# The same instructions in another order of turns on all five engines, with another map of PSUM banks

## The reference

```python
# tokens of an image: stem, deformable convolution, 25 positions of 192
h = leaky_relu(batchnorm(conv2d(x, stem_w, stem_b, 4)))          # 96 x 21 x 21
offset = conv2d(h, off_w, off_b, 4)                              # 32 x 5 x 5
h = leaky_relu(batchnorm(deform_conv(h, offset, dcn_w, dcn_b)))  # 192 x 5 x 5
h = concatenate([h as 25 tokens, txt], axis=1)                   # 102 tokens of 192
# attention with 12 heads of 16, integers by fake_quant, softmax by integer exponent and power of two
h = h + attn(layernorm(h))
# feed-forward, 192 -> 768 -> 192, gelu
h = h + gelu(layernorm(h) @ w_in.T + b_in) @ w_out
```

## Time and profile before

| | |
|---|---|
| median of 3 runs | 1013.89 us (1013.72 to 1017.25) |
| profiled execution, span | 1014.5 us |
| TensorE busy | 880.8 us (87%) |
| VectorE busy | 876.0 us (86%) |
| ScalarE busy | 779.8 us (77%) |
| GpSimd busy | 266.9 us (26%) |
| mean granted TensorE clock | 0.951 |
| transfers | 53.42 MB, mean 53 GB/s |

### The profile page before, as it was taken

One profiled execution on the slowest core, in us unless ns is written; L12 is line 12 of the kernel. 1 busy time (PEld: TensorE's weight loads), 2 busy tenths in 40 slices (PEclk: granted clock), 3 DMA queues, 4 the chain that ended last, 5 costly groups with the idle time before them and its releaser, 6 DMA issues. The chain is left out here.

```text
span 1014.5 us, 18281 instructions
## 1 busy us (share of the span) xinstructions
PE 880.8 (87%) x5594; PEld 539.9 (53%) x5594; DVE 876.0 (86%) x1695; ACT 779.8 (77%) x1529; POOL 266.9 (26%) x248
## 2 busy tenths in 40 slices
...
PEclk9987769999999999999999999999999999998678
...
DMA packets 132628, 53.42 MB, mean 53 GB/s; under 512 B 105103, under 2 KB 131413, under 8 KB 132437
## 3 DMA queue, kind: packets, MB, share of 16 engines
...
## 5 line engine op out<-in xcount | busy, mean ns | idle before, releaser
L563 POOL TENSOR_TENSOR ee_sb<-ee_sb,rs_sb 128x1020 f32<-128x1020 f32 x64 | 157.2, 2464 | 379.1 <-DVE rs_sb L1059 379.1
L1195 PE MATMUL bank<-hats_sb,ht_sb 127*96 127x400 f32 (+1 forms) x384 | 147.9, 522 | 1.7 <-DVE hats_sb L921 1.7
L1327 PE MATMUL bank<-w_out_sb,ge_sb 128*102 128x192 f32 x768 | 138.8, 331 | 10.9 <-DVE y_sb L1096 6.9
L1327 PEld LDWEIGHTS bank<-w_out_sb,ge_sb 128*102 128x102 f32 x768 | 120.3, 168 | 31.6 <-issue 17.8
L921 DVE TENSOR_TENSOR hats_sb<-hats_sb 126x1600 f32<-126x1600 f32 x64 | 127.2, 1987 | 0.7
L648 ACT ACTIVATE hats_sb<-bank 126x400 f32<-126x400 f32 (+1 forms) x256 | 108.2, 523 | 0.3 <-PE bank L1181 0.3
L727 ACT ACTIVATE a_sb<-scores,sc_sb 128x1020 f16<-128x1020 f32 x64 | 71.1, 1111 | 39.2 <-PE scores L1279 39.2
L1195 PEld LDWEIGHTS bank<-hats_sb,ht_sb 127*96 127x96 f32 (+1 forms) x384 | 58.7, 166 | 72.6 <-issue 69.3
L734 ACT ACTIVATE sq_sb<-rm_sb,sc_sb 128x1020 f32<-128x1020 f16 x64 | 73.5, 1148 | 18.2 <-DVE rm_sb L1031 18.0
L572 POOL TENSOR_TENSOR xshift_sb<-mv_sb,xshift_sb 102x4 f32<-102x4 f32 (+1 forms) x33 | 11.0, 333 | 279.9 <-DVE ve_sb L961 278.5
L1242 PE MATMUL bank<-xt_sb,w_in_sb 128*128 128x408 f32 (+1 forms) x204 | 82.0, 527 | 1.0 <-ACT xt_sb L667 1.0
...
## 6 DMA issues: line engine op xcount, KB each, us to landing
...
q_sb<-qb_sb SPq DMA_DIRECT2D x192, 12.8 KB, 1.9
...
```

Source lines behind the costliest of these rows:

```text
L563: nc.gpsimd.tensor_tensor(EE[b][:], EE[b][:], RS[b][:].unsqueeze(2).to_broadcast([128, RT, TOK]), ALU.mult).then_inc(scaled_done, 1)
L1195: last = mm(dst, HT[0:rows, t.i, j, :], HATS[t.i][0:rows, 1 + j, :], start=(j == 0 and not odd), stop=(j == NCH - 2 and odd == 1))
L1327: last = mm(bank[t.banks[0]][0:TOK, 0:D], GE[:, f, t.i * TOK:(t.i + 1) * TOK], WOUT[:, f, :], start=(f == 0), stop=(f == FT - 1))
```

## The change

Each engine has the same set of turns, with the same groups and images meeting in a round, in another order. The lags are written from another origin (the last is 55 instead of 59, PREP0 has -60). In full rounds the order changes as follows; images are those of one round.

The string is replaced as a whole, with the banks:

```diff
-dve.MXB.54 act.XH2.17 pe.INT.9 dve.QQG.55 act.XH2.16 dve.MXC.54 pe.PV3.16 act.V.12 dve.REM.55
...
-dve.PREP2.44
+dve.PW.52 act.HAT.8 pe.PV3.16 dve.PR.52 act.OC.17 dve.RES.55 pe.HTT.6 act.INT.11 dve.LS2.55 sp.QD.20
...
+dve.PR.49 pe.INT.5 act.PV2.13 dve.HAT.42
-BANKS = dict(FFA=(1, 0, 4, 2), STEM0=(5, 4), STEM1=(0, 4), HTT=(5,), OFF=(1,), OFS=(0,), HAT=(5, 0),
-             INT=(3, 2), DCN=(4,), LN1X=(2,), LN2X=(0,), V0=(4, 1), V1=(4, 3), FQ0=(5, 2),
-             FQ1=(0, 4), PV2=(1,), PV3=(4,), FFN0=(5, 3), FFN1=(0, 1), FFN2=(4, 2), FF2=(3,))
+BANKS = dict(FFA=(0, 4, 3, 1), STEM0=(4, 5), STEM1=(3, 5), HTT=(0,), OFF=(4,), OFS=(4,),
+             HAT=(3, 0), INT=(2, 4), DCN=(5,), LN1X=(4,), LN2X=(2,), V0=(2, 3), V1=(1, 3),
+             FQ0=(0, 5), FQ1=(2, 4), PV2=(1,), PV3=(5,), FFN0=(2, 3), FFN1=(0, 1), FFN2=(5, 4),
+             FF2=(2,))
```

More of the change, by code:

```diff
@@ L96 @@
-act.INT.4 pe.INT.6 dve.MXB.51 act.XH2.14 dve.MXC.51 pool.NRM.14 pe.HTT.3 act.LN2X.15 dve.DST.51
-sp.PT.14 dve.BND.51 act.V.9 pe.PV3.13 dve.MAX.50 act.SQ.11 dve.QQ.51 pe.PV2.12 act.LN2X.14
-dve.PREP2.44
+dve.PW.52 act.HAT.8 pe.PV3.16 dve.PR.52 act.OC.17 dve.RES.55 pe.HTT.6 act.INT.11 dve.LS2.55 sp.QD.20
+dve.QKC.48 act.PV2.16 pe.SC.15 pool.RS1.4 dve.HATW.46 act.HTT.7 dve.HAT.45 pe.STEM1.4 act.OC.16
+dve.PV3.54 act.INT.10 dve.HATW.45 pe.SC.14 dve.RES.54 act.SC.15 dve.HAT.44 pe.INT.8 sp.LX.8
+act.VC.15 dve.PV3.53 act.STEM.5 pe.HTT.5 dve.LS2.54 dve.RES.53 act.STEM.4 pe.V1.12 dve.HATW.44
@@ new lines @@
+act.HTT.6 dve.PV3.52 pool.NRM.9 act.SC.14 pe.LN2X.19 dve.LN2A.52 act.INT.9 dve.PREP1.40 sp.SD.16
+pe.SC.13 dve.RES.52 act.INT.8 dve.LS2.53 act.XH2.19 pe.LN2X.18 dve.LS2.52 act.XH2.18 dve.LN2.52
+pe.OFF.4 dve.MAX.51 act.LN2X.19 dve.VE2.52 act.LN2X.18 pe.LN2X.17 dve.MXB.51 act.XH2.17 sp.DCN.16
+dve.MXC.51 pe.DCN.8 pool.NRM.8 act.SQ.15 dve.DST.51 dve.MAX.50 act.V.13 pe.LN2X.16 dve.BND.51
+act.XH2.16 dve.MXB.50 pe.SC.12 act.VC.14 dve.QQ.51 dve.MXC.50 act.VC.13 pe.FFA.16 dve.QQG.51
+sp.YO0.28 act.LN2X.17 dve.DST.50 pe.OFS.4 act.SC.13 dve.EP.51 act.HTT.5 pe.FFN0.16 dve.PREP2.44
```

16 lines of the change are left out of this document (added).

## The result

The changed kernel takes 1028.15 us, median of 4 runs (1025.83 to 1033.8), against 1013.81 us (1011.69 to 1017.25) for four runs of the kernel before: a ratio of 1.0148, 95% interval 1.0114 to 1.0182. The forecast was 1011 us with a range to 1024 us; the time is that of rival 1 (1025 us) and 3 us more. The profiled executions lie closer together than the medians: the changed kernel's was the fastest of its four (1025.83 us, span 1023.7 us), the kernel before's the slowest (1017.25 us, span 1014.5 us), so the traces hold 9 us of the 14 us.

A forecast was written before the change was run, and what follows sets the result against it. A loop between VectorE and ScalarE, closing once per group, was taken to bound the kernel: +0.3 - 0.8 + 0.4 us a group, -1.3 us over 13 groups, -1 us for both ends, so 1011 us; range 1000 to 1024 us.

The forecast's parts named there:

- rival 1: GpSimd's RS1 late in every group, XH1 waits 1.4 us, period 56.15 us: 1025 us; chance 0.22.
- the term for XH1's wait: ScalarE's first XH1 of a group waits for GpSimd's RS1: 0.4 us taken, between 0 and 1.4 us.
- the upper bound of 1.4 us: XH1's wait if RS1's power must sit out EXP too, with RS1 ending at about 579.6 us.
- second half of the loop: LOG.36 to the next QKC: FQ1 ahead of PV2 on ScalarE gives -0.8 us, bounds -0.6 and -1.0 us.
- the +0.3 us for the scores: QKC to LOG.36: VectorE reaches MAX.36 sooner and waits for scores, 0.3 us a group, between nothing and 0.8 us.
- my fourth rival: TensorE falls to its lower clock in other places, some us either way; the clock or something else: chance 0.06.
- HAT.0 starts at 38.9 us: At the start, sooner offset rows are hidden by VectorE's weight preparation; HAT.0 still at 39 us.
- The end: At the end, MXC ahead of QQG may save VectorE 0.5 us.
- HATW of the group's first image: On VectorE, beside GpSimd's NRM.35: HATW.40 loses 0.1 to 1.5 us, none of it on the loop.
- a sign of trouble: A new steady wait on TensorE for a bank or for the gelus would show the forecast wrong.
- The banks at nothing: The new map of PSUM banks costs nothing; every turn finds its bank drained in time, except FF2.
- Rival 2: RS1 and scores in time, freed turns count in full, period 54.45 us: 1003 us; chance 0.30.

The follow-up runs named there:

- experiment 5: Changed kernel with the FF2.28 turn of VectorE moved behind EXP.34 instead of ahead of it: 1008.14 us, ratio 0.9956 to the kernel before.
- experiment 2: Kernel before with VE1 moved behind PR.32, ahead of QQ.35 and EXP.34, as the new order has it: 1049.2 us, ratio 1.0339.
- experiment 1: Changed kernel with VE1 put back directly behind LN1 on VectorE: 1001.72 us, ratio 0.9884 to the kernel before.
- experiment 3: Kernel before with FQ1 directly behind FQ0 on ScalarE, ahead of the PV2 turn: 1010.3 us, ratio 0.9993.
- experiment 8: Kernel before with OFS of group 0 ahead of WDF on GpSimd at the start: 1011.48 us, ratio 0.9973.
- experiment 6: Changed kernel with VE1 half-way back, behind REM.34 and ahead of DST.35: 1004.97 us, ratio 0.9921 to the kernel before.

## Why the prediction was wrong

**The step that failed** is the term for XH1's wait: "Between these ends I take 0.4 us, since the FF2 turn between QQ and EXP.34 reads a PSUM bank and gives GpSimd a gap of 0.3 us." It measured 1.35 us, at the upper bound of 1.4 us that the same passage had. The chain up to there was right: VE1 4.3 us later (4.34 us), and nothing of the margin left if GpSimd isn't let through. What failed is that the FF2 turn would let the power in. FF2 was there, 0.35 us long, the power was issued under it, 0.17 us ahead of EXP.34, and it wasn't let in: it took 3.64 us in all of 13 groups. And I had thought of EXP alone as what holds it, where it was held over four instructions. The upper bound came out right by luck in its cause: it had RS1 done 8.6 us after LN1 and its reader due at 7.2 us, and they came at 8.89 and 7.6 us. Held by EXP alone, RS1 would have ended at about 7.8 us and cost 0.3 us, as in experiment 5. Why a power issued just ahead of EXP waits for four instructions, and one issued just behind its start (experiments 2 and 5) for one, stays open.

**The other terms.** The prediction's second half of the loop rests on QKC of group 10 at 648.56 us, taken from the distance of the two LN1 turns; the trace has it at 648.21 us, so that half was 27.22 us in the round read, not 27.57 us. From QKC to LOG.36 the loop took 28.09 us before and takes 27.79 us in experiment 1 and 28.21 us in the changed kernel (means over 12 groups, those of the other half over 11), so the +0.3 us for the scores wasn't there; VectorE comes to MAX.36 no sooner (12.43 and 12.37 us after QKC). From LOG.36 to the next QKC it took 27.59 us, in experiment 1 26.56 us: -1.03 us, where I had -0.8 us. But the reason was wrong: experiment 3 gives nothing for FQ1's place, and from 200 to 900 us QKC waited for FQ1 only in the round that I had read. That the number is near is luck. The gain arises along the stretch, 0.29 us up to LN1, 0.40 us from there to XH1, 0.34 us to QKC. Changed kernel against experiment 1, that half takes 28.10 - 26.56 = 1.54 us more. That adds up: 0.12 - 1.03 + 1.54 = +0.63 us a group, measured +0.66 us.

**Without a price** was TensorE's clock, my fourth rival, "worth some us either way". It isn't free of the rest: the wait that XH1 hands on brings it. In the new order that is worth some 3.4 us by the profiled execution (5 us, uncertain by 5 us, by the runs), in the old one (experiment 2) about as much as XH1's lateness itself (1.2 against 1.1 us a group). Rival 1 had no such term, but +0.3 us for the scores that mostly wasn't there, and -0.8 us for -1.03 us; its period was to rise by 0.9 us and rose by 0.66 us, and the medians differ by 5 us more than the profiled executions. So its 1025 us lies near the 1028 us partly by luck.

**The ends and the cover.** HAT.0 starts at 38.9 us, as forecast, and experiment 8 confirms that this start is hidden. The end cost 1.2 us instead of giving 0.5 us. HATW of the group's first image fell from 2.56 to 2.00 us, as said, without an effect. FF2's first turn does wait behind the gelus (7.8 us in 12), which I had named as a sign of trouble; in experiment 1 it waits 8.7 us in 13 and the kernel is 1.2% faster, so it is covered. The banks at nothing: the changed kernel's waits of TensorE for a bank are those for FF2's single one (5.7 us in 12, in experiment 1 18.4 us in 26), which the prediction had excepted, and for LN1X's (5.5 us in 9, before 4.3 us in 12). In the old order the map costs 7.9%.

**The rivals.** Rival 2's world is experiment 1: 54.45 us and 1003 us forecast, 54.35 us and 1001.72 us measured. Rival 1's is the changed kernel. The Trainium skill (SBUF — State Buffer, Who interferes with whom) let me derive rival 1 from its strict rule, and its direction was right. But I applied the rule with EXP.34 issued ahead of the power, and in the changed kernel the power is issued first, by 0.17 us, and waits all the same, while EXP keeps its 1.27 us. So the rival came true on a condition that didn't. Where EXP is issued first, in experiments 2 and 5, the power waits for that one instruction, if it ends 0.87 to 1.04 us after it is let in, and these traces agree with the rule; the last multiply of experiment 6, issued behind EXP too, waits over four. I gave rival 1 0.22, against a single favourable argument that no row of the trace had shown; the row that it needed, a GpSimd instruction let in by a turn as short as FF2's, wasn't in what I had read.
